# A decoder layer whose mixture of experts is computed densely for one batch and on sorted tokens for three, on one core

## The reference, cut to what matters

```python
x = x + attn(layernorm(x))            # 16 heads of 64, causal, softmax over the queries
x = x + xattn(layernorm(x), ctx)      # 16 heads of 8
x = x + ffn(layernorm(x))
# ffn: 8 experts, 128 -> 512 -> 128, the best two for each token
scores = x @ Wr + br
_, topk_idx = top_k(scores, 2)
weights = softmax(where(indicator > 0, scores, -inf))
for i in range(8):
    xi = x * indicator[..., i:i+1]
    h = relu(xi @ W1[i] + b1[i])
    out = out + (h @ W2[i] + b2[i]) * weights[..., i:i+1]
```

## Time and profile before

| | us |
|---|---|
| median of 3 runs | 324.39 (324.25 to 325.87) |
| profiled execution | 326.34 |
| its span, first to last instruction | 324.6 |
| mean granted clock of TensorE | 0.989 of full |
| TensorE busy | 297.8 |
| VectorE, ScalarE, GpSimd busy | 206.5, 193.0, 97.8 |

### The profile page before, as it was taken

The page is one execution under the profiler, slowest core; times in us unless marked ns, Lnnn a source line. Parts: engine busy times, 40 slices in busy tenths (PEclk is TensorE's granted clock), DMA queues, the critical chain, the costliest instruction groups (busy, mean ns, idle before and its releaser), DMA issues.

```text
span 324.6 us, 5407 instructions
## 1 busy us (share of the span) xinstructions
PE 297.8 (92%) x1869; PEld 210.2 (65%) x1869; DVE 206.5 (64%) x444; ACT 193.0 (59%) x525; POOL 97.8 (30%) x140
## 2 busy tenths in 40 slices
PE   6789999999989899797989788889999999999995
PEld 2578677877777568453745343436778878678883
DVE  3767657375548885966376673536686867666652
ACT  1569858387747664466276668867655465354451
POOL 7990190035020200720056152055558110000000
PEclk9799999999999999999999999979999999999999
DMA  8900015530100010001084491000000000100001
GB/s 234 210 3 3 1 23 65 67 43 16 36 0 2 16 35 2 5 0 45 5 253 141 112 280 55 3 0 2 0 1 2 0 0 0 35 0 0 2 1 32
DMA packets 14889, 14.06 MB, mean 43 GB/s; under 512 B 2620, under 2 KB 10892, under 8 KB 14860
## 3 DMA queue, kind: packets, MB, share of 16 engines
q1 hardware_dynamic: 13278, 12.92, 16.4%
q10 hardware_dynamic: 1584, 0.80, 0.9%
HBM read 9.94 MB, written 0.52 MB: 32 GB/s over the span
## 4 chain that ended last, share of the span: by engine, by line
PE 73%; DVE 13%; ACT 3%; DMA 3%; issue 3%; SPq 2%; POOL 1%; DVEq 0%; ACTq 0%; POOLq 0%
PE ps L663 7%; PE ps L665 7%; PE ps L664 7%; PE ps L737 6%; PE ps L770 5%; PE ps L782 4%; PE ps L944 4%; PE ps L945 4%; PE ps L946 4%; DVE mneg L1306 4%; PE ps L815 3%; PE ps L852 3%; PE ps L744 2%; SPq L412 2%; DMA w_in<-in_L_attn_W_qkv 2%
## 5 line engine op out<-in xcount | busy, mean ns | idle before, releaser
L1062 ACT ACTIVATE p<-ps,negmax 128x256 f32<-128x256 f32 (+1 forms) x128 | 52.7, 426 | 25.2 <-DVE negmax L1277 24.7
L1392 DVE SCALAR_TENSOR_TENSOR hid_lo<-ps,hid_hi 128x512 fp32r<-128x512 f32 x64 | 43.6, 688 | 33.7 <-ACT hid_hi L1126 33.4
L1306 DVE TENSOR_REDUCE mneg<-ps 128x2 f32<-128x512 f32 x64 | 42.5, 684 | 18.6 <-PE ps L815 18.5
L1126 ACT ACTIVATE hid_hi<-ps 128x512 fp32r<-128x512 f32 x64 | 37.5, 598 | 26.8 <-PE ps L665 26.7
L1092 ACT ACTIVATE px<-ps 128x512 f32<-128x512 f32 x64 | 36.1, 598 | 17.8 <-PE ps L837 17.5
L1277 DVE TENSOR_REDUCE negmax<-ps 128x2 f32<-128x512 f32 (+1 forms) x48 | 32.9, 686 | 19.6 <-PE ps L739 12.5
L815 PE MATMUL ps<-k_st,q_mem 128*128 128x256 bf16 x128 | 24.7, 276 | 9.0 <-DVE mneg L1306 7.6
L504 POOL TENSOR_SCALAR tmp<-mv 128x2 f32<-128x2 f32 x8 | 1.9, 233 | 95.3 <-DVE mv L1301 95.3
L1048 ACT CAST t_hi<-ps 128x512 fp32r<-128x512 f32 x32 | 18.8, 592 | 19.5 <-PE ps L665 18.6
L663 PE MATMUL ps<-x_hi,w_hi 128*128 128x512 f32 x64 | 25.6, 400 | 1.7 <-issue 1.5
L1062 ACT ACTIVATION_READ_ACCUMULATOR p<-ps,negmax 128x1 f32 x128 | 26.6, 208 | 0.0
(11 more groups left out here) (184 smaller groups left out, 663.7 us busy)
## 6 DMA issues: line engine op xcount, KB each, us to landing
w_raw<-in_L_ffn_W SPq DMA_DIRECT2D x2, 1024.0 KB, 6.1
w_last<-in_L_ffn_W SPq DMA_DIRECT2D x8, 256.0 KB, 6.1
k_st<-k_part SPq DMA_DIRECT2D x12, 128.0 KB
q_mem<-q_part SPq DMA_DIRECT2D x48, 32.0 KB
w_in<-in_L_attn_W_qkv ACTq DMA_DIRECT2D x2, 384.0 KB, 6.3
w_in<-in_L_attn_W_qkv SPq DMA_DIRECT2D x2, 384.0 KB, 7.1
resid<-in_x SPq DMA_DIRECT2D x2, 256.0 KB, 4.0
p<-in_L_attn_W_o SPq DMA_DIRECT2D x1, 512.0 KB, 8.3
```

Source lines behind the costliest of these rows:

```text
L1062: last = act.activation(dst, bank[:, n * i:n * i + n], ACT.Exp, bias=negmax[:, kt, h:h + 1], accum_out=psums[:, kt, h:h + 1])
L1126: act.activation(hid[0][:, c, :], ps[:, hidden_banks[NC * k + c], :], ACT.Relu).then_inc(s_ha, 1)
L1306: dve.tensor_reduce(mneg[:, qt, :].rearrange("p (r g) -> p r g", r=2)[:, :, g], ps[:, max_bank[("MX", b, u)], :].rearrange("p (h k) -> p h ...
L1392: dve.scalar_tensor_tensor(hid[1][:, c, :], ps[:, hidden_banks[NC * k + c], :], 0.0, hid[0][:, c, :].bitcast(F32), ALU.max, ALU.subtract). ...
```

## The change

Batch 0 (two token tiles of 128) stays dense: eight tiles `("D", e)` of 256 tokens. The 768 tokens of batches 1 to 3 give 1536 pairs of token and expert. They are sorted by expert into tiles of 256 rows: one for each expert and five spare ones that take an expert's overflow, 13 tiles `("S", j)`, always all computed.

- Order: six dense tiles, the 13 sorted ones (first four experts, then spare ones in turn with the others), two dense ones. A tile is two `H` and two `Y` units, each over two chunks with 256 columns: 24 matmuls. Input rows `X` are made for two tiles at once.
- Routing: `best_two` also marks the experts. `PS` (`ranks`) counts with small matmuls how many pairs of an expert come earlier, `places` computes each pair's row in 18 (first group, batches 1 and 2) or 12 steps on VectorE, `OV` (`spares`) which expert each spare tile has.
- Scatter: GpSimd first writes each norm into `xrow` beside the pair's number (`XC` makes the second copy on ScalarE), then 12 indirect DMAs (`dispatch`) write 128 rows each to a table `xs` in device memory, filled before with padding. SP loads it back as `xr` in three parts. TensorE turns the rows for `X`.
- After a sorted tile, ScalarE adds the second bias (`tile_out`), `YT` turns, VectorE copies (`rows_out`), and two indirect DMAs (`collect`) write the rows to `ys` by pair. At the end SP loads `ys`, and `add_pairs` adds both experts' rows by their weights.
- A spare tile's weights are copied by SP inside on-chip memory, four DMAs of 256 KB from a place read from a register, into one of two buffers.
- Weights are split earlier: units `WS` from group 4 of batch 1, `W2` from group 5 of batch 2, all before the first dense tile. The last rows have eight buffers and no ring. Batch 2's `wo` and batch 3's last `CS` come before the first dense tile, and batch 3 has three score banks.

```diff
-LAST_RING = 3
+LAST_HALF = NE // 2
+DT, ST = TPB, NT - TPB
+PAIRS = 2 * ST * P
+CAP = 256
+SPARE = PAIRS // (CAP + 1)
+NS = NE + SPARE
+ROW = D + 4
+FIRST = 6
+ORDER = tuple(range(NE // 2)) + tuple(j for i in range(SPARE) for j in ((NE + i, NE // 2 + i) if i < NE // 2 else (NE + i,)))
+SEQ = tuple([("D", e) for e in range(FIRST)] + [("S", j) for j in range(NS)] + [("D", e) for e in range(FIRST, NE)])
+ROUTED = ((0, DT), (DT, NT - TPB), (NT - TPB, NT))
...
+        beside = {(0, 0, "h"): [("CO", last, 3)], (0, 1, "h"): [("oq0", last)], (1, 0, "y"): [("oq1", last)],
+                  (1, 0, "h"): [("oT0", last), ("PS", 1)], (1, 1, "y"): [("oT1", last)], (1, 1, "h"): [("wo", last)],
+                  (3, 0, "h"): [("NT", 2), ("XC", 3)], (3, 1, "y"): [("RT", 2)], (4, 1, "y"): [("PS", 2)],
+                  (5, 1, "h"): [("OV", 0)], (10, 0, "h"): [("EX", 1)], (11, 0, "h"): [("GS", 1), ("EX", 2)],
+                  (12, 0, "h"): [("GS", 2)]}
...
+            stack_q(0)
+            sp.wait_ge(s_tab, 1)
+            sp.dma_start(xs.rearrange("(n p) d -> p n d", p=P), pad[:, :].unsqueeze(1).to_broadcast([P, 2 * NS, ROW])
+                         ).then_inc(s_init, 16)
+            for i in range(LAST_HALF):
+                last_rows(i)
...
+            sp.wait_ge(s_xs, 16 * 2 * ST)
+            for i, (n0, n1) in enumerate(XR_PARTS):
+                sp.dma_start(xr[:, 2 * n0:2 * n1, :], xs.rearrange("(n p) d -> p n d", p=P)[:, 2 * n0:2 * n1, :]
+                             ).then_inc(s_xr[i], 16)
...
+            def dispatch(t, c):
+                pool.wait_ge(s_pos, 1 if t < ROUTED[1][1] else 2)
+                pool.wait_ge(s_n3, t + 1) if c == 0 else pool.wait_ge(s_copied, t // TPB)
+                pool.indirect_dma_start(xs, bass.IndirectOffsetOnAxis(pos_i[:, t - DT, c:c + 1], 0),
+                                        xrow[:, t - DT, c, :], None).then_inc(s_xs, 16)
+            def collect(j):
+                pool.wait_ge(s_misc_ev, misc_at[("YT", j)] + 1)
+                for h in range(2):
+                    pool.indirect_dma_start(ys, bass.IndirectOffsetOnAxis(xr[:, 2 * ORDER[j] + h, D:D + 1].bitcast(U32), 0),
+                                            yrow[:, j % 2, P * h:P * h + P], None, bounds_check=PAIRS - 1,
+                                            oob_is_err=False).then_inc(s_ys[j % 2], 16)
...
+            norm_3(3)
+            pool.wait_ge(s_init, 16)
+            for t in range(ROUTED[1][0], ROUTED[2][1]):
+                for c in range(2):
+                    dispatch(t, c)
+            for j in range(NS):
+                collect(j)
...
+                for n in range(2):
+                    c = slice(P * (2 * u + n), P * (2 * u + n) + P)
+                    last = products(ps[:, bank, CAP * n:CAP * n + CAP], w,
+                                    [part[:, x % 2, CAP * half_x:CAP * half_x + CAP] for part in x_p])
...
+            def add_pairs(b):
+                dve.wait_ge(s_yg[b - 1], 16)
+                dve.wait_ge(s_n3, TPB * (b + 1))
+                for c in range(2):
+                    for t in range(TPB * b, TPB * b + TPB):
+                        dve.scalar_tensor_tensor(resid[:, t, :], yg[:, 2 * (t - DT) + c, :], gate[:, 2 + c, t:t + 1],
+                                                 resid[:, t, :], ALU.mult, ALU.add).then_inc(s_sum, 1)
```

More of the change, by code:

```diff
@@ L300, in decoder_layer @@
[L300 to L312, removed]
+                slots.append(slot)
@@ new lines, in decoder_layer @@
+        x_units, i = [], 0
+        while i < len(SEQ):
+            n = 2 if SEQ[i + 1:i + 2] and SEQ[i + 1][0] == SEQ[i][0] else 1
+            x_units.append(tuple(range(i, i + n)))
+            i += n
+        x_of = {i: (x, h) for x, tiles in enumerate(x_units) for h, i in enumerate(tiles)}
+        x_kind = [SEQ[tiles[0]][0] for tiles in x_units]
+        beside = {(0, 0, "h"): [("CO", last, 3)], (0, 1, "h"): [("oq0", last)], (1, 0, "y"): [("oq1", last)],
[3 more added lines that the diff above has]
+                  (12, 0, "h"): [("GS", 2)]}
@@ L481, in _ @@
+            sp.wait_ge(s_misc_ev, misc_at[("YO", 0)] + 1)
+            sp.dma_start(out.rearrange(tiles, p=P)[:, 0:DT, :], resid[:, 0:DT, :]).then_inc(s_out, 16)
+            for b in range(1, B):
+                ts = slice(TPB * b, TPB * b + TPB)
+                sp.wait_ge(s_sum, 2 * TPB * b)
+                sp.dma_start(out.rearrange(tiles, p=P)[:, ts, :], resid[:, ts, :]).then_inc(s_out, 16)
+            sp.wait_ge(s_out, 16 * B)
         @block.gpsimd
@@ new lines, in hidden, with combine @@
+                last.then_inc(s_h, 1)
+            def combine(i, u):
+                kind, at = SEQ[i]
+                j = ORDER[at] if kind == "S" else at
+                bank = ps[:, Y_BANK[kind], 0:CAP]
+                if u == 0 and (kind == "D" or j < NE):
+                    pe.wait_ge(s_w2lo, j + 1)
+                if at == 0 and u == 0:
+                    pe.wait_ge(s_pv_ev, last_in(Y_BANK[kind], ((m, out_bank(m)) for m in range(2 * B))) + 1)
+                    if kind == "S":
+                        pe.wait_ge(s_rank_ev, 2)
+                elif kind == "S" and u == 0:
+                    pe.wait_ge(s_yev, at)
+                pe.wait_ge(s_hd, 2 * i + u + 1)
+                opens = u == 0 and (kind == "S" or j == 0)
+                closes = u == 1 and (kind == "S" or j == NE - 1)
+                for n in range(2):
+                    c = 2 * u + n
+                    if kind == "D" or j < NE:
+                        w = [w[:, NC * j + c, :] for w in w2_p]
+                    else:
+                        w = [ovw[:, j % 2, 2 + k, P * c:P * c + P] for k in range(2)]
+                    h = [part[:, (2 * i + u) % NC, CAP * n:CAP * n + CAP] for part in hid]
+                    pe.matmul(bank, w[0], h[0], start=(opens and n == 0), stop=False)
+                    pe.matmul(bank, w[1], h[0], start=False, stop=False)
+                    last = pe.matmul(bank, w[0], h[1], start=False, stop=(closes and n == 1))
+                last.then_inc(s_y, 1)
```

631 lines of the change are left out of this document (424 added, 207 removed), and 6 rows, old and new, of the table more.

## The result

The changed kernel takes 328.55 us (median of 6 runs, 327.45 to 329.57); the kernel before took 324.39 us beside it (324.05 to 325.87). The ratio is 1.0101, interval 1.0071 to 1.0131 (the two medians alone would give 1.013, the upper end of it): slower by 1.0%, where 320.3 us, 1.3% faster, was forecast. The time lies in the range of 308 to 333, on the other side of no change.

What follows compares the result with a forecast made beforehand. It took the expert stage as TensorE-bound, the new front as bound by VectorE and GpSimd: 221.5 + 36.9 + 52.9 + 1.3 + 7.9 = 320.5 us span, 4.1 less, so 324.39 - 4.1 = 320.3 us; range 308 to 333.

Steps and rivals of the forecast that it cites:

- The start: End of cross-attention, bound by ScalarE: first expert matmul at 221.5 us (219 to 224), against 214.6 before.
- the gap: Between sixth dense and first sorted tile: TensorE idle seven us, waiting for the load of sorted rows.
- rival (c): New front: GpSimd's scatters and VectorE's two-SBUF-input steps disturb each other, 7 us, 327 us in all; chance 0.1.
- the 6.5 us: Cross-attention: ScalarE's added casts, exponentials and copies delay the start by 6.5 us after 214.8, less what three score banks return.
- The scatter: GpSimd's 12 indirect DMAs from 17.3 us after the first expert matmul, 1.1 us each; first sorted matmul at 36.9.
- the norm's time: Front: batch 3's residual and norm queue behind the first ranking (4.2 us); norm done 17.3 us after the first expert matmul.
- Rival (a): Scatters and tiles: indirect DMAs cost 1.9 us each and GpSimd is the bound, 337 us, slower; chance 0.2.
- The front: Six dense tiles with the routing: lasts 30 us on VectorE; TensorE's work of about 22 us doesn't set it.
- Rival (b): Front: routing cheaper, norm by 14, a scatter 0.8 us, so the gap closes, 312 us; chance 0.25.
- The clock: After TensorE's idle time before the sorted tiles: half speed for some microseconds, 1.3 us lost once (0 to 3).
- The sorted tiles: First sorted hidden matmul to last combine: 52.9 us, 3.35 us a sorted tile, matmul starts 0.12 us apart.
- The tail: After the last combine: 7.9 us instead of 4.3, with scatters, gathered rows, 12 additions of 0.23 and output.

Runs made afterwards that it cites:

- run 2: Changed kernel with the first two of GpSimd's 12 scatters ahead of batch 3's norm: 326.65 us, ratio 1.0027 to the kernel before.
- run 3: Changed kernel not waiting for the scattered rows, sorted tiles computed from padding rows, so output incomplete: 319.71 us, ratio 0.9812 to the kernel before.
- run 8: Changed kernel with 50 and 10 needless TensorE products around the first sorted transposes: 327.34 us, ratio 1.0032 to the kernel before.
- run 4: Changed kernel with seven dense tiles in front of the sorted ones instead of six: 327.78 us, ratio 1.0094 to the kernel before.
- run 1: Changed kernel with GpSimd's next three low parts of second expert weights waiting for the batch 0 gates: 325.31 us, ratio 1.0026 to the kernel before.
- run 5: Changed kernel with low parts behind the gates and two scatters ahead of the norm: 323.57 us, ratio 0.9937 to the kernel before.
- run 6: Changed kernel with low parts behind the gates, batch 3's cross-attention output and residual ahead of the first ranking: 328.50 us, ratio 1.0092 to the kernel before.
- run 7: Changed kernel with low parts behind the gates, two scatters ahead of the norm, seven dense tiles in front: 323.36 us, ratio 0.9915 to the kernel before.
- run 9: Changed kernel with low parts behind the gates, two scatters ahead, 36 and 10 needless products around the transposes: 321.50 us, ratio 0.9850 to the kernel before.
- run 10: Kernel of run 9 with four ScalarE casts of second expert weights moved into the first two dense tiles: 323.54 us, ratio 0.9965 to the kernel before.
- run 12: Kernel of run 9 measured again without an edit: 323.05 us, ratio 0.9927 to the kernel before.
- run 13: Changed kernel with 16 and 12 needless TensorE products in two cross-attention waits, gates still held up: 327.78 us, ratio 1.0077 to the kernel before.
- run 14: Kernel of run 9 with 16 and 12 needless TensorE products in two cross-attention waits: 322.34 us, ratio 0.9916 to the kernel before.
- run 11: Changed kernel with four ScalarE casts of second expert weights moved into the first two dense tiles: 327.35 us, ratio 1.0090 to the kernel before.
- the two edits: Low parts behind the gates and two scatters ahead of the norm, both in the changed kernel: 323.57 us, ratio 0.9937 to the kernel before.

## Why the prediction was wrong, point by point

**The start: the step that failed.** "The first expert matmul comes at 221.5 us (219 to 224)" counted ScalarE's added work and nothing else: no hold-up of VectorE and no clock, which the forecast has "lost once", in the gap. With neither hold-up nor drop the runs show 220.3 to 220.4, with the hold-up alone 221.1, which the forecast would have covered; the changed kernel's profile has 224.8, outside the bounds, and those 3.7 us more come with the clock at its lower level twice. What was missed is that moving the second expert weights' split forward puts GpSimd's passes beside the gates, and that TensorE then waits 2.4 us for `o_n`. In four of the five profiles with that wait (the changed kernel, runs 2, 3 and 8, not run 4) the clock falls to its lower level between 212 and 214 us, for 3 to 7 us; in none of the seven without the hold-up (runs 1, 5, 6, 7, 9, 10, 12) is it there at that time. Run 1 removes the hold-up and gives 2.4 us. The forecast had the mechanism, as rival (c) with a chance of 0.1, but looked for it in the new front, beside the scatters. There it did not occur; the ranking steps took 0.17 to 0.23 us, and scatters didn't hold them. The row had shown the real pair, a VectorE step beside a low part of GpSimd, which runs from 240.76 on in the trace of before:

```profile
240.76 1.30 POOL L577 TENSOR_TENSOR w_lo<-w_raw,w_hi 128x512 fp32r<-128x512 f32 x1
```

The Trainium skill (SBUF — State Buffer, Who interferes with whom) says that VectorE and GpSimd lock each other out both where a VectorE step has two SBUF inputs and where it is in a mode that takes both pairs of ports, which a `tensor_scalar` can enter. By that, the trace agrees for the masks, held at 1.83 us; it also has the `tensor_scalar` held at 1.19 us, but no profile shows in which mode that ran. Only the first kind was in the forecast.

ScalarE as the sole bound there was also too much: four of its casts are worth 0.8 us (run 10). That the 6.5 us came out near the truth (5.7 to 5.8 from 214.64, without hold-up and drop) is in part luck, since other waits took part. The forecast's own terms, 214.8 and 6.5 less what three score banks give back, also add up to less than 221.3, not to 221.5.

**The scatter.** 1.1 us each was forecast, 1.26 measured, inside the bounds of 0.66 to 1.9. From the first scatter to SP's load 16.5 us against 15.1, the load 3.2 against 2.4, transposes and the rest 2.5 against 2.1; the first scatter started 0.8 earlier than said, at 16.5. The place of the gap, its length and its cause were right, and runs 2 and 3 show them. The reason given for the norm's time was right by half: the first ranking delays it by some 2 us, not by 4.2 (run 6). Rival (a) is out: GpSimd's 26 collects are 25.6 us of work with 35.5 us of idle time before them, 29.3 of it waiting for VectorE's copy of the rows, so the tiles set their pace. Its bound of 333 us does not follow from its own terms: at 1.7 us each they give 329.4, with a start at 224 331.9.

**The front.** 30 us forecast, 29.0 measured (run 3). Rival (b), no gap, is out.

**The clock.** 1.3 us forecast, 2.1 measured in the gap by run 8. A second drop, before the experts, wasn't forecast. In the profiles it follows on TensorE's waits and is absent when they are filled (runs 13 and 14). After the 2.4 us that the hold-up brings it comes mostly, as counted above. After the next wait, of 1.3 to 1.8 us for ScalarE's exponentials near 217 us, it comes in six profiles (the changed kernel, runs 2, 6, 7, 8, 9) and not in seven (runs 1, 3, 4, 5, 10, 11, 12), whatever the gates do; what decides that is open. In one kernel it made an execution 3.6 us longer (runs 9 and 12); what it costs the median is open (run 13).

**The sorted tiles.** 52.9 us forecast, 53.3 measured with a full clock. Matmuls start 0.12 apart, spare weights are not awaited, and a tile takes 3.42 us where 3.35 were forecast. TensorE's own work nearly fills it; the loop over ScalarE and VectorE adds little: once in two tiles a combine starts 0.36 us after the matmul ahead of it and not 0.12, right behind its low part on VectorE. Right.

**The tail.** 7.9 us forecast, 9.3 measured. The step "12 additions of 0.23" is mis-sized: they take 3.86 us together, 0.32 each, which is 1.1 of the 1.4.

**The balance.** Of the forecast's 4.1 us gain, the start took 3.3, gap and clock 2.6, the tail 1.4. The sorted tiles themselves were worth what was said; all four terms around them came out on the dear side of the value taken. With the two edits and the filled gap the span is 319.0 us in a fast execution, and the time about 1.1% below before.

## What to carry to other kernels

When work is moved forward on one engine, list what the shared consumers do at its new place: each of GpSimd's full-width passes over SBUF that met VectorE's small steps held one of them until its end, about 1 us, so put them where VectorE reads PSUM (low parts of the hidden units kept their 0.69 us beside such passes) or waits. Ask too what the engine behind it then waits for: here the clock mostly fell after TensorE's wait of 2.4 us. A round trip through device memory by indirect DMAs has its price (here 12 issues of 1.26 us, landing, 3.2 us of load); start it as soon as the first rows are known; to put tiles into the gap gave almost nothing, since they then no longer cover the second trip at the end. Before reordering an engine's queue, look at whether the steps ahead fill a wait: of the ranking's 4 us half did. And compare two executions only after a look at the clock of both.

## What the runs showed of the hardware

- An indirect DMA of 128 rows takes GpSimd 0.96 us (1.26 for the first) and 0.30 to the next, with rows of 528 bytes; with rows of 512 bytes 0.98 and 0.30. Beside the 12 scatters the second ranking's steps on VectorE took 0.15 to 0.23 us, as without them.
- A `tensor_scalar` on 128x2 elements took 1.19 us beside a GpSimd pass over 128x512, 0.17 without. It holds the other way too: two norm passes of GpSimd, 0.91 us together when alone, took 1.42 us beside VectorE's low part of x in run 1.
- Needless products in TensorE's idle time before the sorted tiles kept the clock at 1.00 there; the profile is 2.1 us shorter behind the landing of the rows, the ratio 0.7% better.
- The same kernel with the clock at 0.50 from 218 to 228 us has a span of 322.6 us, with the clock up 319.0.
- In the gap of 6.87 us the clock fell between 258 and 259 us, and it stayed at 0.50 until 268 us, with TensorE at work from 260.97 on.
